# Two f32 products split into three f32r products each, with a high part by ScalarE and a low part by GpSimd

## The reference

```python
def _sq_relu(h):
    return jnp.square(jax.nn.relu(h))

x = x + attn_a(layernorm(x))            # linear attention, 16 heads of 16
x = x + ffn(layernorm(x))               # the block of this change
x = x + attn_b(x)                       # acts on the first 16 tokens of a batch alone; elsewhere it adds its bias ob
x = x + ffn(layernorm(x))

def ffn(x):                             # shared part: (1024*8, 256) @ (256, 128) @ (128, 256)
    out_shared = _sq_relu(xf @ Ws1) @ Ws2
    ...                                 # eight routed experts, whose weight is trunc(softmax of top 2)
```

## Time and profile before

| | |
|---|---|
| device time, 3 runs | 404.89, 405.32, 406.13 us, median 405.32 |
| the profiled execution | 404.83 us, span of its instructions 403.1 us |
| granted clock of TensorE | 0.997 of full speed |
| PE busy | 381.8 us, 95% of the span |
| DVE, POOL, ACT busy | 295.9, 250.6, 233.1 us |
| chain that ended last | PE 70%, DVE 16%, issue 5%, POOL 4%, ACT 3% |

### The profile page before, as it was taken

The page is one execution under the profiler, slowest core; times in us unless marked ns, Lnnn a source line. Parts: engine busy times, 40 slices in busy tenths (PEclk is TensorE's granted clock), DMA queues, the critical chain, the costliest instruction groups (busy, mean ns, idle before and its releaser), DMA issues.

```text
span 403.1 us, 7255 instructions
## 1 busy us (share of the span) xinstructions
PE 381.8 (95%) x2458; PEld 312.0 (77%) x2458; DVE 295.9 (73%) x674; ACT 233.1 (58%) x402; POOL 250.6 (62%) x306
## 2 busy tenths in 40 slices
PE   7889999999999999989889999999999999989993
PEld 4778989998999898877677777676877776676762
DVE  5688786778677866784894589689658768875574
ACT  3587886788678867444455565444545354364451
POOL 4488886788678865577455658596437846745402
PEclk9999999999999999999999999999999999999998
DMA  8921111111100000122533033302330231231103
GB/s 246 265 91 53 54 53 54 54 53 54 54 0 2 0 2 2 52 89 59 162 112 103 13 108 111 110 25 88 108 95 27 101 111 32 80 109 56 42 14 113
DMA packets 29497, 29.78 MB, mean 74 GB/s; under 512 B 5622, under 2 KB 25340, under 8 KB 29436
## 3 DMA queue, kind: packets, MB, share of 16 engines
q1 hardware_dynamic: 28876, 28.50, 22.9%
q10 hardware_dynamic: 560, 0.52, 0.5%
HBM read 19.98 MB, written 8.98 MB: 72 GB/s over the span
## 4 chain that ended last, share of the span: by engine, by line
PE 70%; DVE 16%; issue 5%; POOL 4%; ACT 3%; DMA 1%; SPq 0%; DVEq 0%; POOLq 0%; ACTq 0%
PE PB L1583 8%; DVE ln_bn L1110 4%; PE PA L1653 4%; PE PA L1659 3%; PE PA L1654 3%; PE PT L1630 3%; PE PG L1434 3%; PE PG L1429 3%; PE PG L1430 3%; PE PT L1343 2%; PE PT L1665 2%; DVE x_all L1164 2%; PE PA L1606 2%; PE PB L1388 2%; PE PA L1388 2%
## 5 line engine op out<-in xcount | busy, mean ns | idle before, releaser
L534 POOL TENSOR_TENSOR o_lo<-q_all,o_hi 128x512 fp32r<-128x512 f32 x32 | 40.2, 1279 | 38.3 <-ACT o_hi L812 38.3
L517 POOL TENSOR_TENSOR xn_pair<-scratch,xn_pair 128x512 fp32r<-128x512 f32 x32 | 41.8, 1307 | 30.6 <-ACT xn_pair L655 30.6
L1583 PE MATMUL PB<-ws,scratch 128*128 128x256 f32 x240 | 58.8, 388 | 1.5 <-DVE x_all L1172 1.3
L1583 PEld LDWEIGHTS PB<-ws,scratch 128*128 128x128 f32 x240 | 43.6, 190 | 15.6 <-issue 10.6
L1110 DVE BATCH_NORM_STATS2 ln_bn<-x_all 128x6 f32<-128x256 f32 x128 | 44.9, 412 | 0.9
L510 POOL TENSOR_TENSOR x_all<-x_all,wvo 128x1024 f32<-128x1024 f32 x16 | 45.3, 2831 | 0.0
L526 POOL TENSOR_TENSOR q_all<-q_all,scratch 128x512 f32<-128x512 f32 x32 | 41.1, 1304 | 0.1
L936 DVE TENSOR_TENSOR o_lo<-scratch,o_hi 128x512 fp32r<-128x512 f32 x32 | 32.7, 1023 | 4.2 <-ACT o_hi L673 2.7
L1164 DVE TENSOR_TENSOR x_all<-PA,x_all 128x1024 f32<-128x1024 f32 x16 | 19.6, 1222 | 20.9 <-PE PA L1659 20.9
L819 ACT ACTIVATE scratch<-PB,ln_rsq 128x256 f32<-128x256 f32 x28 | 11.7, 470 | 39.3 <-issue 21.8
L1429 PE MATMUL PG<-xn_pair,o_hi 128*128 128x256 f32 x128 | 32.1, 285 | 2.0 <-ACT o_hi L673 2.0
(11 more groups left out here) (280 smaller groups left out, 1122.7 us busy)
## 6 DMA issues: line engine op xcount, KB each, us to landing
scratch<-inv_scratch SPq DMA_DIRECT2D x32, 256.0 KB
x_all<-n_L_attn_a_inputs_q_dram SPq DMA_DIRECT2D x15, 512.0 KB, 3.5
out_dram<-x_all SPq DMA_DIRECT2D x15, 512.0 KB, 5.7
inv_scratch<-inv_turned SPq DMA_DIRECT2D x16, 32.0 KB
out_dram<-x_all SPq DMA_DIRECT2D x2, 256.0 KB, 2.3
x_all<-n_L_attn_a_inputs_q_dram ACTq DMA_DIRECT2D x2, 128.0 KB, 2.7
x_all<-n_L_attn_a_inputs_q_dram SPq DMA_DIRECT2D x2, 128.0 KB, 2.9
setup<-in_L_attn_a_Wq_dram ACTq DMA_DIRECT2D x1, 256.0 KB, 4.9
```

The lines of the kernel that those rows point to most:

```text
L517: nc.gpsimd.tensor_tensor(halves[:, :, 1, :], pair(xn[n % 2], h), halves[:, :, 0, :].bitcast(F32), ALU.subtract).then_inc(x_lo, 1)
L534: nc.gpsimd.tensor_tensor(o_lo[:, c, :], q[:, c, :], o_hi[:, c, :].bitcast(F32), ALU.subtract).then_inc(o_lo_done, 1)
L1583: last = mm(four(dst)[:, t, :], h[:, t * P:(t + 1) * P], ws2[:, :], start=(t % 2 == 0 and not onto_rows), stop=True, skip_group_check=True)
```

## The change: an f32r split of `h2s`, `wc` and `ws2`

An f32 matmul stands in the trace as two passes; an f32r matmul is one. Each of the two f32 products with `h2s` is replaced by three f32r products: high x high, high x low and low x high. The high part `h2_hi` is a rounding copy on ScalarE, put behind `lay_ob` and ahead of slot 2, of `m_high(B - 1)` in step 1 and of `query_high(i + 1)`; the low part `h2_lo` is a difference on GpSimd, put behind L624 and ahead of slot 2 and `query_low(i + 1)`. On TensorE the two inner products with `h2_hi` and the eight down products with it come first, then slot 3, then the one inner and the four down products with `h2_lo`. `f2_mm` still counts the two halves, `f3_mm` the inner product. The weights are split once, in step 0, by ScalarE and VectorE. `token_of` moves into a used piece of `q_all` to make room.

```diff
@@ GpSimd, step
                     nc.gpsimd.tensor_tensor(last, last, y3[:, by_dve(v):T, :], ALU.add).then_inc(out_pool, 1)
+                if runs(r):
+                    pool.wait_ge(h2_hi_done, r + 1)
+                    ge(pool, f2_mm, 2 * r)
+                    nc.gpsimd.tensor_tensor(h2_lo[:, :], h2s, h2_hi[:, :].bitcast(F32), ALU.subtract).then_inc(h2_lo_done, 1)
                 chain(i, 2)
@@ ScalarE, step 0 and step
+                nc.scalar.activation(ws2_hi[:, :], ws2[:, :], ACT.Copy).then_inc(ws2_hi_done, 1)
...
-                nc.scalar.activation(wc, PT[:, 0, 0:F], ACT.Copy).then_inc(fold_sb, 1)
+                act.wait_ge(bo_added, NG)
+                nc.scalar.activation(wc_hi[:, :], PT[:, 0, 0:F], ACT.Copy).then_inc(fold_sb, 1)
...
                     lay_ob(i, r, v)
+                    act.wait_ge(f1_scaled, r + 1)
+                    ge(act, f2_mm, 2 * r)
+                    nc.scalar.activation(h2_hi[:, :], h2s, ACT.Copy).then_inc(h2_hi_done, 1)
                 if i == NG:
                     scale_tiles(i, v)
                 chain(i, 2)
@@ VectorE, step 0
+                    dve.wait_ge(ws2_hi_done, 1)
+                    nc.vector.tensor_tensor(ws2_lo[:, :], ws2[:, :], ws2_hi[:, :].bitcast(F32), ALU.subtract).then_inc(wc_lo_done, 1)
...
+                if i == 0:
+                    dve.wait_ge(fold_sb, 4)
+                    nc.vector.tensor_tensor(wc_lo[:, :], PT[:, 0, 0:F], wc_hi[:, :].bitcast(F32), ALU.subtract).then_inc(wc_lo_done, 1)
@@ TensorE
+            def inner_high(r):
+                pe.wait_ge(h2_hi_done, r + 1)
+                for w in (wc_hi, wc_lo):
+                    mm(PT[:, 0, :], w[:, :], h2_hi[:, :], start=False, stop=False, skip_group_check=True)
+            def down_high(r):
+                pe.wait_ge(ob_laid, r + 1)
+                for t in range(T):
+                    for w in (ws2_hi, ws2_lo):
+                        mm(four(PB)[:, t, :], h2_hi[:, t * P:(t + 1) * P], w[:, :], start=False, stop=False, skip_group_check=True)
+            def inner_and_down_low(r):
+                pe.wait_ge(h2_lo_done, r + 1)
+                mm(PT[:, 0, :], wc_hi[:, :], h2_lo[:, :], start=False, stop=True, skip_group_check=True).then_inc(f3_mm, 1)
+                for t in range(T):
+                    last = mm(four(PB)[:, t, :], h2_lo[:, t * P:(t + 1) * P], ws2_hi[:, :], start=False, stop=True, skip_group_check=True)
+                    if t % 2 == 1:
+                        last.then_inc(f2_mm, 1)
...
                 if runs(r):
-                    pe.wait_ge(f1_scaled, r + 1)
-                    mm(PT[:, 0, :], wc, h2s, start=False, stop=True, skip_group_check=True).then_inc(f3_mm, 1)
+                    inner_high(r)
+                    down_high(r)
                 chain(i, 3)
                 if runs(r):
-                    pe.wait_ge(ob_laid, r + 1)
-                    down(PB, h2s, f2_mm, True)
+                    inner_and_down_low(r)
                     run_experts(r, nr, i)
```

More of the change, by code:

```diff
@@ L170, in hybrid_kernel @@
         w1c = part(C * F).rearrange("p (c f) -> p c f", c=C)
-        wc = part(F)
         l_blk = [part(P) for _ in range(3)]
@@ L184, in hybrid_kernel @@
         kvt = [g[:, 0:C * P].rearrange("p (c n) -> p c n", c=C) for g in g_flat]
-        token_of = sb("token_of", [P, B * P])
+        ws2_hi, ws2_lo = sb("ws2_hi", [P, D], F32R), sb("ws2_lo", [P, D], F32R)
+        h2_hi, h2_lo = sb("h2_hi", [P, GT], F32R), sb("h2_lo", [P, GT], F32R)
+        wc_hi, wc_lo = sb("wc_hi", [P, F], F32R), sb("wc_lo", [P, F], F32R)
         PT, PA, PB, PG = ps("PT"), ps("PA"), ps("PB"), ps("PG")
@@ L218, in hybrid_kernel @@
         xs, xsub = used_q[1](D, SP), used_q[1](D, SP)
+        token_of = used_q[1](B * P)
         lin, kc, vi = [used_q[2](D, SP) for _ in range(3)]
@@ L277, in hybrid_kernel @@
         fold_mm, fold_sb, w1c_ready = [sem(n) for n in ("fold_mm", "fold_sb", "w1c_ready")]
+        ws2_hi_done, wc_lo_done, h2_hi_done, h2_lo_done = [sem(n) for n in ("ws2_hi_done", "wc_lo_done", "h2_hi_done", "h2_lo_done")]
         stored = sem("stored")
@@ L1578, in fold_ffn_product, with down @@
                 last.then_inc(fold_mm, 1)
-            def down(dst, h, done, onto_rows):
+            def down(dst, h, done):
                 for t in range(T):
[L1583 to L1586, removed]
+                    last = mm(four(dst)[:, t, :], h[:, t * P:(t + 1) * P], ws2[:, :], start=(t % 2 == 0), stop=True, skip_group_check=True)
+                last.then_inc(done, 1)
+            def inner_high(r):
[14 more added lines that the diff above has]
+                        last.then_inc(f2_mm, 1)
             def row_scales(i):
@@ L1621, in step @@
                         pe.wait_ge(f2_added, 2 * (v + 1))
-                    down(f4_pair(v), h3, f4_mm, False)
+                    down(f4_pair(v), h3, f4_mm)
                 chain(i, 1)
@@ L1626, in step @@
                         pe.wait_ge(fold_sb, 4)
+                        pe.wait_ge(wc_lo_done, 2)
                     ge(pe, f3_relu, r)
```

## The result

The changed kernel takes 414.5 us (median of four runs, 412.42 to 414.9) where the kernel before, on the same chip, takes 405.11: the ratio is 1.022, with an interval of 1.0195 to 1.0245. Forecast were 410.7 and a range of 405.5 to 414.0. The sign was right and the size too small. The profiled execution took 414.62, with a span of 412.9 for 403.1.

What follows compares the result with a forecast made beforehand. The prediction saw equally long TensorE and VectorE paths bounding plain tails. Its terms, -1.4 + 1.4 + 3.3 + 2.1 = +5.4 on the profiled 404.83, gave 410.2, stated as 410.7 for the median; range 405.5 to 414.

Steps and rivals of the forecast that it cites:

- What bounds the kernel: Plain tail: TensorE's path (4.01 us) and VectorE's (4.04) meet at the next down product, so TensorE's 0.48 saving gains nothing.
- forecast idle time of half a microsecond: Plain tail: TensorE idles half a microsecond behind transposes and norm product, until VectorE's second addition is done.
- TensorE's gains of 1.4: Tails with slot 3, such as steps 3, 8 and 9: shorter products gain down to VectorE's floor, -1.4 us in sum.
- steps 11 and 12: Tails of these two steps: a gain of 0.2 us together, since step 12 stands after a power on GpSimd.
- Steps 1 and 2: ScalarE's copy, queued ahead of the attention matrix, delays VectorE by 1.3 us; with step 2's inner product, +1.4 in sum.
- the later inner product of step 2: Step 2: the copy adds 0.65 us before the first inner product; shorter products and slot 3 take about 0.55 back.
- Steps 5 to 8: GpSimd's power slips behind the low part, `variances` of step 7 behind it, TensorE waits: +3.3 us in sum.
- VectorE is held up by the new difference: Rival, chance 0.2: GpSimd's difference blocks VectorE in steps 5 and 7, one full hold of 1.28 us each, 413.3 us.
- smaller slip of GpSimd's queue: Step 5: a smaller slip of the same kind as GpSimd's delayed power and statistics in step 6, 0.1 us.
- Step 16: The end: GpSimd's low part is queued behind its addition to x, and all that is left waits: +2.1 us.

Runs made afterwards that it cites:

- run 5: Changed kernel with VectorE writing its product straight as `h2_hi`, copy and difference left out, low products reading `h2_hi` (result incomplete): 404.58 us, 0.9988 of the kernel before.
- run 2: Changed kernel with ScalarE's `m_high(B - 1)` ahead of the copy `h2_hi` in step 1: 412.2 us, 1.0167 of the kernel before.
- run 4: Changed kernel with 14 idle f32r products each ahead of step 2's high inner product and step 16's low products: 412.51 us, 1.0168 of the kernel before.
- run 3: Changed kernel with GpSimd's power ahead of the low part in step 6 alone: 412.3 us, 1.0162 of the kernel before.
- run 1: Changed kernel with GpSimd's low part ahead of its half addition to x in step 16 alone: 412.21 us, 1.015 of the kernel before.
- run 12: Changed kernel with low part first in steps 5 and 16, matrix first in step 1, power first in step 6, 14 idle products in step 2: 406.72 us.

## Why the prediction was right in sign and wrong in size

- **What bounds the kernel: right.** Two paths of equal length, of which the chain names one. TensorE's forecast idle time of half a microsecond is there (0.48), and run 5 puts the products alone at 0.1% for the 7.7 us of saving. TensorE's gains of 1.4 came out at about 0.8 (from the ruler to the end run 5 is 219.37 for 220.19): the tail of step 10 took 0.3 back, where a VectorE operation met more of a GpSimd one, and 0.2 forecast for steps 11 and 12 did not come.
- **Steps 1 and 2: the queue was right, the step that failed first is the price of the wait.** The sum has 1.3 for `h2_hi` ahead of the matrix and 0.1 net for the later inner product of step 2. The first measured 1.28, and run 2 takes it back. With the clock kept (run 4) step 2 to 3 is 0.18 longer than before, so the second was right as well, for the wait as such. It priced that wait by its length alone and left out 1.6 us of lower clock behind it.
- **Steps 5 to 8: the mechanism was right, the size was not.** Power behind low part, `variances` behind both, TensorE waiting for the high part of step 7: all seen; 3.2 was forecast for it, 2.48 measured, and run 3 puts the power's place in the queue at 2.0.
- **Step 5: the second step that failed; the rival came true there.** "VectorE is held up by the new difference" had 0.2 of the chance, with one full hold in each of two steps. In step 5 it came: the operation went from 1.94 us to 3.20, 1.26 for the 1.28 of a full hold. The smaller slip of GpSimd's queue, put at 0.1, was 0.53; together the stretch became 1.79 longer. In step 7 no such hold shows: with the power in its old place (run 3), step 7 to 8 is 0.49 longer, as much as `variances` are later there. That rival and the forecast were not alternatives, and the sum had to carry both.
- **Step 16: right in place, and short by the clock.** 2.1 forecast, 2.85 measured; 0.74 is the lower clock (run 4), the other 2.1 the late low part, as forecast (run 1 takes 2.5 back in all).

Together, from the table: 1.7 more in step 2, 1.7 in step 5, 0.75 at the end and 0.6 of gains that did not come, less 0.7 in steps 5 to 8, make 4.1 of the 4.2 between +5.4 and +9.58. About 2.4 of it is the clock and 1.3 the hold; the backlog that was put too high hid 0.7 of the rest. Four moves and one fill take back all but 0.9 in the profiled execution and all but 1.5 by the medians (run 12).

Open stays what decides whether a given wait lowers the clock. Shown is that filling it keeps the clock, and that the same wait at another time leaves it. One run of the changed kernel took 412.42 us with a mean clock of 0.989 for 0.984; that fits one fall fewer, but it has no profile.

## What to carry to other kernels

Before work is moved off a busy engine, look for the second path that ends at the same place: here it was 0.03 us away, and a saving of 7.7 us was worth 0.1%. An operation that is added to an engine with idle time costs what stands behind it in that engine's queue, and where it is GpSimd's, what VectorE does beside it (1.3 us in step 5). Order mends most of that: the operation that the bound engine waits for goes first, and what waits for a transfer does not move ahead of it.

## What was not expected of the hardware

- TensorE's granted clock fell to about half (0.58 and 0.56 over 4 us in the changed kernel) behind waits of 1.9 us in the middle of dense work and came back by itself; behind waits of 1.8 to 2.1 us that ended 0.5 us earlier or 1.2 us later and more it did not fall. That is four of seven executions in step 2.
- A VectorE operation of 0.40 us on 64x256 numbers took 1.94, 3.20 and 4.41 us as GpSimd ran two, three and four operations behind each other beside it, the last a memset: it ended with the memset and not between the others, though GpSimd went on behind it without a pause.
